# Small-head attention on one core: score matmuls moved to the end of a place, with one wait for both head pairs

## The reference, cut to what matters

```python
def sdpa(q, k, v, mask):
    scores = jnp.einsum('bhqd,bhkd->bhqk', q, k) / np.sqrt(HD).astype(np.float32)
    scores = jnp.where(mask, scores, jnp.float32(-1e+30))
    probs = jax.nn.softmax(scores, axis=-1)
    return jnp.einsum('bhqk,bhkd->bhqd', probs, v)
...
x = x + global_latent_attn(rmsnorm(x, norm1_w), g_wq, g_kv_down, g_k_up, g_v_up, g_wo)
x = x + local_gqa_attn(rmsnorm(x, norm2_w), l_wq, l_wk, l_wv, l_wo)
```

## Time and profile before

| | |
|---|---|
| median of 3 runs | 1894.65 us (1891.13 to 1906.78) |
| profiled execution, its own time | 1895.89 us |
| its span | 1894.0 us |
| mean granted TensorE clock over the span | 0.912 |
| busy, share of the span | PE 1579.9 us (83%), PEld 1119.3 (59%), DVE 1262.7 (67%), ACT 1053.6 (56%), POOL 978.2 (52%) |
| the stage of the change, 720 to 1028 us | PE busy 268.21 us of 308, DVE 183.75, ACT 149.31, POOL 114.23; granted clock 0.83 |
| scores, all | 1024 matmul records, 121.8 us busy |
| exponentials, all | 256, 132.5 us busy; ACT idle before them 142.1 us, 139.9 of it for the scores |

### The profile page before, as it was taken

One profiled execution on the slowest core, in us unless ns is written; L12 is line 12 of the kernel. 1 busy time (PEld: TensorE's weight loads), 2 busy tenths in 40 slices (PEclk: granted clock), 3 DMA queues, 4 the chain that ended last, 5 costly groups with the idle time before them and its releaser, 6 DMA issues. The chain is left out here.

```text
span 1894.0 us, 37662 instructions
## 1 busy us (share of the span) xinstructions
PE 1579.9 (83%) x13094; PEld 1119.3 (59%) x13094; DVE 1262.7 (67%) x3810; ACT 1053.6 (56%) x2749; POOL 978.2 (52%) x738
## 2 busy tenths in 40 slices
PE   5999997889999878899887789999976667939795
PEld 4999995556666543344444466666644545626564
DVE  3555554898888744655764798888825987737454
ACT  3655663788888744556433588888842112315332
POOL 1333332988778622324443788787813665542036
PEclk9999998999999987999757999999987888969788
DMA  5000000111111100000000111111100000210012
GB/s 212 1 1 1 1 1 4 29 34 28 28 31 27 26 7 1 1 1 2 1 1 1 25 31 31 32 28 27 33 6 1 0 1 12 46 33 1 1 40 28
DMA packets 41081, 38.62 MB, mean 20 GB/s; under 512 B 21944, under 2 KB 32192, under 8 KB 40512
## 3 DMA queue, kind: packets, MB, share of 16 engines
q1 hardware_dynamic: 35264, 32.02, 6.5%
q0 software_dynamic: 5632, 4.20, 1.8%
HBM read 13.14 MB, written 4.20 MB: 9 GB/s over the span
## 5 line engine op out<-in xcount | busy, mean ns | idle before, releaser
L995 ACT ACTIVATE arena<-ps 128x512 f32<-128x512 f32 (+5 forms) x680 | 366.8, 571 | 311.8 <-PE ps L332 94.5
L1235 ACT ACTIVATE arena<-ps 128x320 f32<-128x320 f32 (+4 forms) x256 | 132.5, 561 | 142.1 <-PE ps L683 139.9
L1151 ACT ACTIVATE arena<-arena,g_small 128x128 f32<-128x128 f32 x512 | 197.8, 391 | 0.5
L2221 POOL TENSOR_TENSOR arena<-arena,consts 128x512 f32<-128x512 f32 (+1 forms) x64 | 93.2, 1456 | 186.8 <-ACT arena L1235 186.7
L1707 DVE CUSTOM_DVE_ANT_0 arena<-ps,consts,g_ss 128x128 f32<-128x128 f32 x512 | 146.8, 341 | 43.3 <-PE ps L526 43.3
L683 PE MATMUL ps<-arena 32*128 32x160 f32 (+4 forms) x1024 | 121.8, 466 | 14.4 <-SPq L2502 4.8
L2271 POOL TENSOR_TENSOR g_ss<-g_ss,consts 128x8 f32<-128x8 f32 x64 | 108.2, 1691 | 44.2 <-DVE g_ss L1737 40.5
L332 PE MATMUL ps<-consts,arena 128*128 128x128 f32 x400 | 76.4, 324 | 56.2 <-DVE arena L1495 13.8
L2332 POOL TENSOR_TENSOR arena<-arena 128x2048 f32<-128x2048 f32 x16 | 86.9, 5442 | 56.7 <-ACT arena L1257 56.7
L1579 DVE TENSOR_REDUCE arena<-arena 128x8 f32<-128x1032 f32 x32 | 39.3, 1228 | 110.4 <-ACT arena L1052 110.4
L2192 POOL TENSOR_TENSOR arena<-arena,consts 128x8 f32<-128x8 f32 x32 | 52.7, 1648 | 114.2 <-DVE arena L1579 114.2
(11 more groups left out here) (257 smaller groups left out, 4240.1 us busy)
## 6 DMA issues: line engine op xcount, KB each, us to landing
arena<-arena SPq DMA_DIRECT2D x112, 128.0 KB, 2.3
weights<-in_w SPq DMA_DIRECT2D x1, 5069.0 KB, 24.4
weights<-in_w SPq DMA_DIRECT2D x1, 2052.0 KB, 12.8
arena<-Y SPq DMA_DIRECT2D x64, 32.0 KB
arena<-Y SPq DMA_DIRECT2D x64, 31.8 KB
consts<-in_c SPq DMA_DIRECT2D x1, 1278.0 KB, 8.8
sorted_rows<-X SPq DMA_DIRECT2D x1, 1024.0 KB, 5.1
X<-sorted_rows SPq DMA_DIRECT2D x4, 256.0 KB, 3.6
```

The source lines that it names most:

```text
L995: copy = lambda o, i: act.activation(o, i, ACT.Copy)
L1151: last = act.activation(g_p[:, n % 2, 4 * hf + i, :], g_sc[:, 4 * hf + i, :], ACT.Exp, scale=-1.0, bias=g_mn[:, h:h + 1], accum_out=g_rs[: ...
L1235: act.activation(b_p[:, U % 2, 2 * gp:2 * gp + 2, at:at + n], ps[:, b:b + 2, 0:n], ACT.Exp, scale=float(HD) ** -0.5).then_inc(s.b_exp, 1)
L2221: pool.tensor_tensor(v, v, m.unsqueeze(1).broadcast_to([P, NG, n]), ALU.mult)\
```

## The change

In `scores`, both pairs wait for the count 8U + 2j, that is for all exponentials of the places before, where pair 0 waited for one fewer. In the loop on TensorE, the two calls of `scores` move from the head of the place to its end, behind `finish`, `prepare` and `values`. The other engines' streams are unchanged.

```diff
@@ scores
-                    need(pe, s.b_exp, st - 1)
+                    need(pe, s.b_exp, 8 * U + 2 * j)
@@ small_heads, the loop of TensorE
                     for j in range(NT):
-                        if U < 32:
-                            scores(U, j, 0)
-                            scores(U, j, 1)
                         finish(U, j)
                         if U < 28:
                             prepare(U // NR + 1, NR * (U % NR) + j)
                         if 1 <= U <= 32:
                             values(U - 1, j)
+                        if U < 32:
+                            scores(U, j, 0)
+                            scores(U, j, 1)
```

## The result

| | before | after |
|---|---|---|
| median | 1895.02 us (1891.13 to 1906.78, 4 runs) | 1964.44 us (1959.96 to 1967.33, 4 runs) |
| profiled execution, span | 1895.89, 1894.0 | 1966.84, 1965.0 |
| mean granted TensorE clock | 0.912 | 0.885 |
| the stage, first S to S(31,3) | 300.7 | 374.6 |
| global half, local half | 168.62, 132.06 | 223.83, 150.75 |

The ratio after to before is 1.0354, interval 1.0302 to 1.0405: slower, where 1941 us, ratio 1.0245, was forecast. The profiled execution grew by 71.0 us; the stage grew by 73.9 and everything outside it shrank by 2.9. So the place was right and the stage's +46.5 was too small by 27.4.

A forecast was written before the change was run, and what follows sets the result against it. TensorE was taken to bound the global half, preparation on DVE and POOL units 16 to 27. Global +35, units 16 to 27 +1.5 and units 28 to 31 +10 gave +46.5 on 1894.65: 1941 us, range 1916 to 1980.

The forecast's parts named there:

- The bound: TensorE sets the pace in the global half, busy 35.48 of 38 us at full clock.
- (e): Whole stage: added idle TensorE time could push the clock to 1.2 GHz; no separate amount in the sum.
- (a): Score pairs: pair 1 no longer starts late, up to 0.9 us less TensorE time in a split place.
- The check: Sign in the profile after: TensorE's busy time in the stage falls as split pairs go, while the stage grows.
- (b): From scores to scores: the later of TensorE's work and second exponential's end + 0.05; clean global unit 8.99, +0.95 us.
- (c): Global half: finish and prepare steps waiting for ACT lose their cover; units 8 to 11 +10.2, half +35 us in all.
- (d): Local half: DVE's copy delays place 1's transposes; units 28 to 31 +10 (27.0 full clock, 34 lower), 16 to 27 +1.5.
- the third rival: Clock falls to 1.2 GHz for the stage: clean global unit about 12.0, total about 2000 us; chance 0.08.
- The first: Rival: TensorE's own work decides, place 0 to 1 taking 2.45; faster, 1860 us; chance 0.06.
- E1: The second of a place's two exponentials on ACT; at width 512 it ends 3.11 us after the scores began.
- The second: Rival: the wait falls into slack of DVE's and POOL's chains; no change, 1895 to 1912 us; chance 0.12.
- The range's high end: 1980 us, taking the low clock in half of the stage.

The follow-up runs named there:

- the old order: Only the joined wait put into the kernel before, scores still first in a place: 1893.14 against 1895.45 us, ratio 1.0003.
- the order with V first: Joined wait added to the order with values ahead of scores, except one late place per four units: 1895.41 against 1891.41 us for the kernel before, ratio 1.0022.
- both filled: Repeated values in TensorE's stalls, against the kernel before: changed kernel 1939.81 us, ratio 1.0279; new order with the old wait 1918.24 us, ratio 1.013.
- filled: Changed kernel with place 0's values computed again in TensorE's known stalls: 1939.81 against 1895.45 us for the kernel before, ratio 1.0279.
- its filled form: Kernel before with place 0's values repeated in the stalls of units 19, 23 and 27: 1888.18 against 1891.41 us, ratio 0.9983.

## Why the prediction was right, and where it was short

**The bound.** Right: TensorE set the pace in the global half, and taking its work behind ACT's reading cost time there. In the profiled execution the stage grew by 73.9 where +46.5 was summed; the step that fell short is (e), the clock, below.

**(a) Joining.** Right in kind: the splits are gone, and where nothing else changes TensorE's busy time falls, 35.25 to 32.61 in units 8 to 11. The check that it would fall *in the changed stage* failed: 280.3 us for 263.5, since the lower clock makes the same matmuls longer.

**(b) The joined wait.** Right as a mechanism: 3.16, 2.52, 1.88 in the changed kernel, 8.82 for a clean unit where 8.8 was expected in the old order, and 9.01 against the 8.99 computed in unit 10 of the order with V first. Its sum over the half, 16 times 0.95, is 15.2; on top of the new order, both filled, it measured 14.1, a part of which may be clock, and 3.2 for 3.8 in units 8 to 11, where the clock was full. As a price of the wait alone it would have been wrong: +0.4 in the old order.

**(c) The order.** Right at full clock, in units 8 to 11: 4.43, 4.89, 3.84, 7.42 and 9.57 stand against 4.51, 4.88, 3.82, 7.54 and 9.59, and +10.2 for the four against +10.5. The other cycles were never seen at full clock: filled, they gave +5.6 for +7, +8.7 for +10 and, in units 12 to 15, +11.2 for +7.4, with 10 us of that cycle at the lower clock; unfilled the last gave +9.4.

**(d) The local half.** Units 16 to 27 +3.8 for +1.5, inside its bounds of -10.5 and +9. Units 28 to 31 took 35.44 us, nearly all at 1.2 GHz, where 27.0 was computed for full clock and 34 for the lower one: the upper end was sound, the middle that was taken was not, and no run of this kernel with its DVE link shows the lower end. The link through DVE's copy was rightly seen.

**(e) The clock: the term that was mis-sized.** The prediction gave it nothing in the global half's sum beyond units 0 to 3, on the ground that TensorE would still work three quarters of the time, and kept it for the range and the third rival. In units 8 to 11 it measured 9.0 us (57.35 against 48.31 filled). In the global half the filling gave back 19.2 (223.83 against 204.66), of the 20.2 by which that half was off, and not the whole clock, since 47 us stayed at 1.2 GHz; that the two numbers nearly meet is partly luck, as the cycles above show. The local half was off by 7.2 (18.7 for 11.5), and the filling gave back 5.4. It was not the third rival either, 1.2 GHz throughout: the half stood at 0.76, with units 12 to 15 nearly whole. What should have spoken was in the earlier trace rows: the local stretch, idle 6.2 of 40 us, stood at 0.63, and (c)'s own sum gave units 8 to 11 10.2 us in which TensorE had nothing new to do, with the 2.5 of before 12.7 idle us of 48. The page "TensorE: Matmul & The Clock Gate" of the Trainium skill, section "HAM oscillation — how this bites in real kernels", describes such a loop, whose gaps let the clock drop so that the burst behind each gap starts slow, and advises keeping the engine busy; the rows here agree (2.05 for 1.16 behind a gap, 9.0 us back from the filling), for gaps made by a semaphore instead of the page's DMA waits.

**The rivals.** The first fell as said: E1 is later than TensorE's own work wherever the rows said so, and only halved exponentials gave its 2.45 (2.44). The second, hidden in other engines' slack, is false for the change and true for the wait alone. The third's 12.0 for a clean unit at 1.2 GHz does not follow from its own terms: 9.0 with 0.9, 0.7 and 0.5 more, and a last place of twice 1.43, is 11.6, so +42 in place of +48. The range's high end, 1980, took the low clock in half of the stage; it had it in 204 of 374.6 us (before in 99 of 300.7), and 1964 lies in the range only because that end allowed for it.

## What to carry to other kernels

Put behind a producer's output the work that needs nothing from its reader, and ahead of everything that waits for one; a wait is cheap or dear by what stands next to it (+0.9 or +3.2 us in the same 38), so price the pair, not the line. When a sum adds idle time to TensorE in a stretch at full clock, work the stretch out at both clocks and let the size of the new gaps choose between them, for the clock can cost nearly as much as the gaps (9.0 and 10.5 us in units 8 to 11). And before an instruction is moved to the front, list what it waits for itself.

## What was not expected of the hardware

- Idle times of 2.17, 0.82 and 1.29 us within 13 us were followed by matmuls at 1.2 GHz, in a stretch that before stood at 1.00 with 2.5 us of idle time in 38. Two, one and three repeats in this cycle's three stalls were enough to keep 1.00.
- The clock is not the same in every execution. Of the 13 executions of the kernel before beside the first experiments, the fastest, 1878.06 us, had a mean clock of 0.920 and the slowest, 1903.12, one of 0.903; in every series of four or more executions on record the longer times go with the lower clocks. So the spread of this kernel goes with the clock; what changes the clock from one execution to the next was not shown.
- The same instructions can take either clock. Units 28 to 31 are identical in the kernel before and in its filled form, and begin within 0.01 us of each other, behind units that are not identical; they took 20.52 us at clock 1.00 in the one profile and 26.80 at 0.68 in the other.

The first row is the kernel before's:

```profile
1000.30:1020.82 20.52, 19.91 (x269) 12.22 (x269) 12.29 (x21) 11.48 (x31) 12.52 (x8) 1.00 0.01 2
```

and this is its filled form's:

```profile
1000.29:1027.09 26.80, 26.37 (x269) 15.59 (x269) 11.27 (x21) 11.65 (x31) 12.42 (x8) 0.68 0.00 1
```

So a price read from one profile of the local half can be off by some 6 us for this alone.
